# Context tiles turned over two steps, a running maximum begun on ScalarE, projections by pass, and the last normalisation in another block

## The reference

```python
# x (8, 56, 512), ctx (8, 1500, 512), mask (8, 56, 1500), 32 query heads, 8 key and value heads of 128
n = layernorm(x)
q = rope(heads(n @ wq)); k = rope(repeat4(heads(ctx @ wk))); v = repeat4(heads(ctx @ wv))
p = softmax(q @ k.T / sqrt(128) + mask)
x = x + tanh(g_xattn) * (merge(p @ v) @ wo)
flat = layernorm(x)
gates = softmax(keep_top2(flat @ Wr.T))                  # 4 experts
x = x + tanh(g_ffn) * sum_e gates[e] * ((flat @ A[e].T) @ B[e].T)
```

## Time and profile before

| what | us |
|---|---|
| median of 3 runs (lowest, highest) | 1941.91 (1937.64, 1943.05) |
| the profiled execution | 1944.6 |
| its span, first to last instruction | 1942.7 |
| TensorE busy | 1863.1 |
| VectorE busy | 1552.9 |
| GpSimd busy | 1194.0 |
| ScalarE busy | 1019.1 |

### The profile page before, as it was taken

The page is one execution under the profiler, slowest core; times in us unless marked ns, Lnnn a source line. Parts: engine busy times, 40 slices in busy tenths (PEclk is TensorE's granted clock), DMA queues, the critical chain, the costliest instruction groups (busy, mean ns, idle before and its releaser), DMA issues. The chain is left out here.

```text
span 1942.7 us, 36348 instructions
## 1 busy us (share of the span) xinstructions
PE 1863.1 (96%) x12454; PEld 1706.5 (88%) x12454; DVE 1552.9 (80%) x2598; ACT 1019.1 (52%) x1882; POOL 1194.0 (61%) x990
## 2 busy tenths in 40 slices
PE   7989999999999999999999999999999999999688
PEld 7979998999889998999899988999899988999576
DVE  6768888888878888888888888888788888888244
ACT  5645555555555555555655555555455555556232
POOL 5627666666666674777566666776576656777300
PEclk9999999999999999999999999999999999999788
DMA  6622111112111111221112211111121110211270
GB/s 221 251 73 37 36 21 32 26 37 31 31 32 34 32 16 33 37 36 21 31 26 36 31 23 30 32 35 20 31 32 31 30 33 13 56 16 21 60 249 20
DMA packets 75303, 91.98 MB, mean 47 GB/s; under 512 B 22948, under 2 KB 49828, under 8 KB 75144
## 3 DMA queue, kind: packets, MB, share of 16 engines
q1 hardware_dynamic: 74136, 83.44, 20.2%
q10 hardware_dynamic: 1008, 6.42, 0.8%
HBM read 74.07 MB, written 15.77 MB: 46 GB/s over the span
## 5 line engine op out<-in xcount | busy, mean ns | idle before, releaser
L699 POOL TENSOR_TENSOR pT<-prob,pT 125x448 fp32r<-125x448 f32 x384 | 483.8, 1271 | 86.1 <-ACT pT L824 86.1
L881 PE MATMUL low_banks<-wv_hi,cT_hi 128*125 128x256 f32 x1536 | 434.4, 283 | 0.0
L881 PE MATMUL low_banks<-wv_hi,cT_lo 128*125 128x256 f32 x1536 | 432.7, 282 | 0.0
L881 PE MATMUL low_banks<-wv_lo,cT_hi 128*125 128x256 f32 x1536 | 432.3, 281 | 0.0
L765 ACT ACTIVATE k_work<-low_banks 64x500 f32<-64x500 f32 x384 | 223.8, 583 | 193.3 <-PE low_banks L865 186.1
L1081 DVE TENSOR_TENSOR prob<-t_banks,mask_t 125x448 f32<-125x448 f32 x384 | 235.3, 618 | 110.2 <-PE t_banks L916 95.4
L693 POOL TENSOR_TENSOR k_lo<-k_work,k_hi 128x500 fp32r<-128x500 f32 x192 | 253.8, 1322 | 110.1 <-ACT k_hi L773 110.1
L865 PE MATMUL low_banks<-cT_hi,wk_hi 128*128 128x500 f32 x768 | 315.5, 411 | 0.4 <-DVE cT_lo L1052 0.4
L710 POOL TENSOR_TENSOR sums<-sums,prob 125x448 f32<-125x448 f32 x252 | 291.0, 1155 | 26.8 <-ACT prob L818 25.8
L865 PE MATMUL low_banks<-cT_lo,wk_hi 128*128 128x500 f32 x768 | 298.8, 389 | 0.0
L865 PE MATMUL low_banks<-cT_hi,wk_lo 128*128 128x500 f32 x768 | 298.5, 389 | 0.0
(11 more groups left out here) (152 smaller groups left out, 3857.0 us busy)
## 6 DMA issues: line engine op xcount, KB each, us to landing
stage<-in_ctx_dram SPq DMA_DIRECT2D x72, 250.0 KB
inv_b<-inv_by_head SPq DMA_DIRECT2D x65, 112.0 KB, 4.8
attn_by_head<-attn SPq DMA_DIRECT2D x65, 112.0 KB, 1.7
wq_raw<-in_L_xattn_wq_dram SPq DMA_DIRECT2D x7, 1024.0 KB, 6.8
q_raw<-q_by_head SPq DMA_DIRECT2D x64, 112.0 KB, 4.9
head_rows<-in_ctx_dram SPq DMA_DIRECT2D x24, 250.0 KB
stage<-in_L_xattn_wo_dram SPq DMA_DIRECT2D x4, 1024.0 KB, 6.9
k_work<-in_L_xattn_wo_dram SPq DMA_DIRECT2D x4, 1024.0 KB, 7.7
```

What stands on the lines that cost most here:

```text
L699: nc.gpsimd.tensor_tensor(pT[:, j % PT_SLOTS, :, 1, :], pair(j), f32(pT[:, j % PT_SLOTS, :, 0, :]), ALU.subtract).then_inc(p_lo, 1)
L881: mm = nc.tensor.matmul(v_banks[0:ST, m % 2, t * PAIR:(t + 1) * PAIR], cT[a][:, d, tile * ST:(tile + 1) * ST], w[1][mv][:, d, g * DH:g * D ...
```

## The change

All lists of words are written anew. Beside that:

- A new kind of step, "ahead", takes the place of "even" in the step before the turn (step 6). The context tiles 0 to 5 of the next batch are turned there, tiles 6 to 11 in the turn, and the mask behind the keys of the turn. The loads of tiles 9 to 11 wait for tiles 0 to 2 as before, which are now one step earlier.
- A word copy on ScalarE (begin_top) writes the first pair of scores to the running maximum's bank; top 1 on VectorE then takes the maximum of that bank and the second pair, as the others do. Each of the 64 steps has one copy more.
- The first two projections go by pass over all heads: O p h is pass p of head h of the first group, R p pass p of the second group for all its heads. Pass 0 needs the high halves alone. GpSimd's low halves of wo are spread over the step before the last.
- The inverse sums of the last step, their way through DRAM and the normalisation with them go to the beginning of output_part; the loads of the third and fourth group follow the last step's store on SP directly.

```diff
 PE_STEP
-    "odd": ("K00 K01 Y K02 X K03 M K10 K11 K12 K13 V00 K20 K21 K22 PV0 K23 V01 PV1 V10 S0 S1 PV2 S2 V11 V20 S3 "
-          "V21 S4 PV3 PV4 S5 PV5"),
+    "odd": ("K00 K01 K02 K03 K10 Y X K11 M K12 V00 K13 V01 PV0 K20 K21 K22 K23 PV1 V10 S0 V11 S1 V20 S2 PV2 PV3 "
+          "S3 V21 S4 PV4 PV5 S5"),
-    "turn": ("W0 W1 C0 X C1 M C2 C3 V00 Y C4 K00 C5 K01 C6 K02 K03 C7 C8 PV0 V01 K10 K11 K12 C9 K13 V10 C10 C11 "
-           "V11 PV1 S0 S1 K20 K21 K22 K23 S2 PV2 S3 V20 V21 PV3 PV4 S4 S5 PV5"),
+    "ahead": ("K00 K01 K02 K03 Y C0 X K10 K11 M C1 C2 K12 V30 K13 C3 C4 V31 K20 K21 K22 PV0 PV1 K23 S0 V40 S1 PV2 "
+            "V41 S2 S3 PV3 V50 C5 V51 S4 PV4 S5 PV5"),
+    "turn": ("K00 C6 C7 K01 K02 K03 X C8 C9 M K10 V00 C10 K11 K12 V01 K13 Y C11 V10 PV0 PV1 K20 K21 W0 W1 K22 K23 "
+           "PV2 S0 V11 S1 V20 S2 S3 V21 S4 PV3 S5 PV4 PV5"),
-    "last": "X O00 M O01 Y O02 O03 PV0 PV1 PV2 PV3 PV4 PV5 Y1 O1",
+    "last": "O00 O01 X O02 O03 M O10 O11 Y O12 O13 O20 O21 O22 O23 R0 PV0 PV1 PV2 R1 R2 PV3 PV4 PV5 Y1",
...
 ACT_STEP
+    "pre": ("Q swap0 exp0 hi0 exp1 exp2 hi1 swap1 exp3 khi0 hi2 vhi3 khi1 swap2 wo0 hi3 exp4 vhi4 hi4 exp5 khi2 "
+          "copy0 vhi5 attn0 hi5 olo"),
+    "last": "exp0 hi0 exp1 hi1 exp2 hi2 wo1 attn1 exp3 exp4 exp5 hi3 hi4 hi5 wo2 attn2 olo",
...
 DVE_STEP
-    "odd": ("comb mred qlow sub0 sub1 sin0 cos0 rot0 sub2 cos1 sin1 rot1 sub3 sub4 yred sin2 sub5 cos2 rot2 mask0 "
-          "mask1 vlow0 mask2 top1 top2 mask3 vlow1 top3 vlow2 mask4 norm top4 mask5 top5 oadd"),
+    "odd": ("comb mred sub0 sub1 cos0 sub2 sin0 rot0 yred sub3 sin1 sub4 qlow cos1 rot1 sin2 sub5 vlow0 mask0 "
+          "cos2 rot2 norm mask1 mask2 top1 top2 mask3 vlow1 top3 vlow2 mask4 oadd top4 mask5 top5"),
...
 POOL_STEP
+    "odd": "lo0 sum1 lo1 klow0 lo2 sum2 sum3 klow1 lo3 klow2 lo4 lo5 sum4 sum5 fin",
+    "pre": "lo0 sum1 lo1 sum2 klow0 sum3 lo2 lo3 klow1 lo4 wo0 klow2 lo5 sum4 sum5 fin wo1 wo2 wo3",
...
 def step_kind(g, last):
-    return ("last" if last else "turn") if g == HKV - 1 else ("odd" if g % 2 else "even")
+    ends = ("pre", "last") if last else ("ahead", "turn")
+    return ends[g - HKV + 2] if g >= HKV - 2 else ("odd" if g % 2 else "even")
...
+        def begin_top(n, item):
+            act.wait_ge(t_free, item + (RING + 1))
+            if n > 0:
+                act.wait_ge(subbed, n * PT)
+            nc.scalar.activation(run_max, pair(0), ACT.Copy).then_inc(top_begun, 1)
...
         def top(n, item, j):
             dve.wait_ge(t_free, item + (RING + 1))
-            if j > 1:
+            if j == 1:
+                dve.wait_ge(top_begun, n + 1)
+            else:
                 dve.wait_ge(topped, n * (PT - 1) + j - 1)
-            nc.vector.tensor_tensor(run_max, pair(0) if j == 1 else run_max, pair(j), ALU.max).then_inc(topped, 1)
+            nc.vector.tensor_tensor(run_max, run_max, pair(j), ALU.max).then_inc(topped, 1)
...
+def project_part(nc, shared, part, h, u, first):
+    a, m = PASSES[part]
+    for c in range(DC):
+        mm = nc.tensor.matmul(shared.low_banks[:, c, 0:TOK], shared.wo_s[a][:, u, h, c * P:(c + 1) * P],
+                              shared.attn_s[m][:, u, h].rearrange("p b s -> p (b s)"), start=first, stop=False,
+                              skip_group_check=True)
+    return mm
...
 attention_part, SP
         batch(B - 1, True)
-        spread_inverse(B, 0)
         output_loads(sp, shared, wo, attn_dram, 0, sp_passed)
-        store_attn(B, 0)
...
 attention_part, VectorE
-        split_low(nc, dve, shared, 2, 0)
-        normalise(B, 0)
...
 output_part, SP
-        for u in range(2):
-            sp.wait_ge(shared.attn_stored[u], 16 * (B * (HKV // 2) + 1 + u))
+        spread_inverse(nc, sp, shared, inv_dram, B, 0)
         sp.dma_start(x_tok[:, :, :], x_v).then_inc(x_loaded, 16)
...
-        with sp.Fori(1, pairs - 1) as i:
-            output_loads(sp, shared, wo, attn_dram, i, sp_passed)
+        output_loads(sp, shared, wo, attn_dram, 1, sp_passed)
+        store_attn(sp, shared, attn_dram, B, 0)
+        for u in range(2):
+            sp.wait_ge(shared.attn_stored[u], 16 * (B * (HKV // 2) + 1 + u))
+        output_loads(sp, shared, wo, attn_dram, 2, sp_passed)
...
 output_part, VectorE
         split_low(nc, dve, shared, 3, 1)
+        normalise(nc, dve, shared, B, 0)
```

More of the change, by code:

```diff
@@ L157, in t_item, with context_item @@
 def t_item(b, g, what, n, last):
-    kind = step_kind(g, last)
-    return b * BATCH_FILLS + (FIRST_FILLS + g * STEP_FILLS + t_place(kind, what, n))
+    before = sum(len(t_fills(PE_STEP, step_kind(e, last))) for e in range(g))
+    return b * BATCH_FILLS + (FIRST_FILLS + before + t_place(step_kind(g, last), what, n))
+def context_item(b, m):
+    g = HKV - 2 if ("C", m) in t_fills(PE_STEP, "ahead") else HKV - 1
+    return t_item(b, g, "C", m, False)
 def s_item(b, g, j):
```

145 lines of the change are left out of this document (78 added, 67 removed), and 52 rows, old and new, of tables (ACT_STEP, DVE_STEP, PE_STEP, POOL_STEP).

## The result

The changed kernel takes 1990.97 us (median of 4 runs, 1987.33 to 1997.6) against 1942.08 us before: a ratio of 1.026, 95% interval 1.0227 to 1.0293. It is slower by 49 us, where 13 were forecast, and lies 6 us above the range. Its profiled execution took 1988.8 us with a span of 1987.3, 44.6 us more than the span before.

What follows compares the result with a forecast made beforehand. Ordinary steps were taken as bound by TensorE's own work, with waits at turns and the end. Terms -35 (turns) + 67 (odd steps) - 18.5 (end) = +13.5 us gave 1955 us, range 1889 to 1985.

Steps and rivals of the forecast that it cites:

- the stall: Odd steps: TensorE waits 2.8 us before S3 behind the moved-up normalisation; +67 us in 24 steps (31 to 105).
- covered: Rival, odd steps: the normalisation's wait is covered, the 67 us go; 1888 us, chance 0.23.
- half-covered: Rival, odd steps: inverse earlier and GpSimd out of the way, so part of the wait goes; 1924 us, chance 0.12.
- the fit: Inverse sums' transfers: 2.0 us plus bytes at 436 GB/s each, so odd steps would cost nothing; the forecast rejected it.
- the rival: Odd steps: the gap pulls TensorE's clock down to 1.2 GHz in half of them, +24 us; 1979 us, chance 0.10.
- Turns: Step ahead and turn: the new context tile order removes waits and two turns' lower clock; -35 us over seven turns.
- The end: Last steps and output block: 19.3 us gained up to TensorE's second block, about 1 lost later; net -18.5 us.
- The running maximum: ScalarE's copy saves VectorE 0.8 us a step, but TensorE covers it: 0, at worst 0.3 us a step.
- the tiles' term: Context tiles in step ahead and turn: 4.4 us gained a turn, 31 in seven; with clock recovery -35 us.
- the likeliest case: The forecast itself, whole kernel: 1955 us, chance 0.50, said to run from 1932 to 1983 by its wait's bounds.

Runs made afterwards that it cites:

- late normalisation: Changed kernel with the odd steps' normalisation moved back from behind the first masking to behind the fifth: 1885.61 us, ratio 0.9733.
- no wait: Changed kernel, lists untouched, odd steps' normalisation neither using nor waiting for the inverse sums: 1885.82 us, ratio 0.974.
- gap filled: Changed kernel with TensorE's odd list ending V21 PV4 PV5 S3 S4 S5, normalisation left in place: 1948.54 us, ratio 1.0016.
- one masking later: Changed kernel with the odd steps' normalisation behind the second masking instead of the first: 1926.93 us, ratio 0.9919.
- before, moved up: Kernel before the change with the odd steps' normalisation moved from behind the fifth masking to behind the first: 2153.25 us, ratio 1.1078.
- the end alone: Kernel before with only the change's end (projections by pass, last normalisation in output block, wo low halves by head): 1924.69 us, ratio 0.9904.

## Why the prediction was wrong

**Odd steps: the stall was right.** The forecast had the inverse 12.0 us behind the reciprocal, a stall of 2.8 us in front of S3, 67 us in all. Measured: 11.9 to 13.1 us in the first two odd steps of each batch and 11.1 to 11.6 in the third, gaps of 1.64 to 3.81 us, 2.69 on the mean, 64.5 us together. One run left the word in its place and took the wait away, one left VectorE's wait and filled TensorE's gap, and one moved the word. The covered and half-covered rivals fall. By an estimate from the fit that I set against the stall, which the Trainium skill (DMA: Bandwidth & Descriptors, section "Anatomy of one DMA — SWDGE (gpsimd) path") gives for GpSimd's path, both transfers would have been done in 4.3 us. The trace of the changed kernel has medians of 6.7 and 4.8 us for them on SP's queue, so the fit does not carry over to these.

**The step that failed: the clock.** The sum put nothing for it, and the rival had half of the odd steps, 24 us, at a chance of 0.10. In fact 19 of 24 fell, in 20 stretches (one step has two). Steps with the same gap of 2.7 us last 28.25 us at full clock (2 of them) and 29.67 below it (13); those of 1.65 us 26.83 (3) and 28.60 (2). Set against the same steps of the late normalisation, the five at full clock lost their gap and 0.2 us more; the other nineteen lost 30 us beyond that, 1.5 us a stretch. With it the sum comes out: -34.3 (ahead and turn) + 64.5 (gaps) + 5.3 (24 times the 0.2 us) + 30 (clock) - 20.7 (end) = 44.8, against 44.6 measured. The forecast's 13.5 and these 30 make 43.5; all its other misses nearly cancel.

What misled me was the row of the turn with its 2.22 us gap at a mean clock of 1.00. Five turns of that trace had this gap and stayed at full clock, but the two that fell had longer ones:

```profile
541.66 0.65 PE L892 MATMUL t_banks<-ident,stage 125*128 125x125 f32 x4 [2.46 <-DVE cT_lo L1052]
...
1391.56 0.65 PE L892 MATMUL t_banks<-ident,stage 125*128 125x125 f32 x4 [2.77 <-DVE cT_lo L1052]
```

The second is the 2.8 us that I forecast for the odd steps. Nor was 2.22 us safe: in the two later kernels that keep the turn list of before, it was followed by the lower clock 8 times of 13. A gap and the lower clock behind it were not a case beside the forecast but a term of it, and its chance should have stood on the count of rows, not on one of them. The steps of all these kernels, by their longest single gap:

| gap, us | steps | of these below full clock |
|---|---|---|
| none (odd steps: late normalisation; no wait) | 48 | 0 |
| 0.3 to 1.0 (gap filled) | 24 | 3 |
| 0.35 to 0.75 / 1.75 (one masking later) | 19 / 5 | 0 / 1 |
| 1.64 to 1.72 (changed kernel) | 5 | 2 |
| 2.7 (changed kernel) | 15 | 13 |
| 3.8 (changed kernel) | 4 | 4 |
| 6.0 to 7.1 (before, moved up) | 24 | 24 |
| 2.22 / 2.46 and 2.77 (turns: before) | 5 / 2 | 0 / 2 |
| 2.2 to 2.3 (turns: moved up; the end alone) | 13 | 8 |
| 1.1 (one turn of the end alone) | 1 | 0 |

**Turns: right.** -35 us were forecast, -34.3 measured; step ahead and turn last 56.8 us together, and no wait of TensorE for a context low half is left in them. All fourteen run at full clock. What the normalisation reached in the turn was not the fifth scores but the low half of the last values (L920, 1.4 us in seven turns); the turn is 0.6 us longer for it (29.0 us beside 28.4 above), inside the 1.0 that I left.

**The end: the mechanism right, the size partly by luck.** From the last X to the output block 25.4 us are gained and 1.1 lost in the step before, 24.3 where 19.3 were worked out. Half of these 5 us is the third group's first load, for which I took 8.5 us from the row of before, where the last inverse sums were being loaded beside it; now ScalarE could begin 6.0 us after its issue:

```profile
1881.79 0.38 SPq L268 DMA_DIRECT2D stage<-in_L_xattn_wo_dram  x1
...
1887.77 1.91 ACT L1255 ACTIVATE wk_hi<-stage 128x2048 fp32r<-128x2048 f32 x1 [7.87 <-DMA stage<-in_L_xattn_wo_dram]
```

The output block gives back 3.7, where I had put 1, with 3 as the high end; 2.8 of it is TensorE's wait for the fifth group (the row of L1280 above). Net -20.7 against -18.5: two misses of opposite sign.

**The running maximum: a zero that was a gain.** I let 0.8 us of VectorE a step count for nothing since TensorE covers it on the mean of a step. It does in the 48 even and odd steps. In the step ahead the maximum stands ahead of the last keys' rotation, and 0.49 us of it come through. Without the copy 10 us were lost in all, so at least 3.4 of the 34.3 us that I booked to the tiles are its own, and the tiles' term agreed with mine partly by chance.

**Numbers that do not follow.** By the bounds that I gave the stall, 31 to 105 us, the likeliest case runs from 1919 to 1993 us, not from 1932 to 1983, and the 1991 measured would have lain inside. That would have been luck, since the stall came out near its middle and the clock made the rest. The half-covered case saves 0.9 and 0.4 us, so 1.3 us a step and 31 in all, which gives the -17.5 that I wrote; 1.5 and 36 do not. And the two long turns were not 2 us longer by the clock alone: 0.24 and 0.55 us of it are their longer gaps.

## What to carry to other kernels

Before a word is moved up in an in-order list, write down when its input arrives, which instructions stand behind it, and which of them another engine needs first; the answer is an addition of a few rows, and on the mean it held to 0.1 us a step here. Price a stall of TensorE with the clock that it may cost, as a term and not as a case: here the gaps cost 65 us and the clock behind them another 30. When a large change comes out slower, move single words of it back before it is given up: one of them turned 1.026 into 0.973.
